# The products, copies and transfers of a batch laid out anew: first x turned by TensorE, q copied by ScalarE, three buffers of Q, K twice in the weight

## The reference, cut to what matters

```python
xn = layernorm(x)
q  = (xn @ Wq.T + bq) * 16 ** -0.5              # 16 x 512 x 256
k, v = split(xn @ Wkv.T + bkv)                  # 16 wide each
qr = q.reshape(16, 16 * 512, 16)                # 8192 rows of queries a batch
attn = softmax(qr @ k.T) @ v                    # the bulk: 8192 x 512 a batch
out_a = attn.(heads back) @ Wo.T + bo
tokens = einsum('elr,erc->elc', A, B)           # 6 experts x 100 tokens
a = softmax(xn @ tokens.T / 16)                 # kept for the chosen expert only
delta = (a[..., 1:] @ val[1:] + xn) @ wd.T + wd_b
out_f = xn + log(exp(delta * scale))            # of the chosen expert
result = x + out_a + out_f
```

## Time and profile before

| | |
|---|---|
| median of 3 timed runs | 1049.19 us (1047.77 to 1050.99) |
| profiled execution, its own time | 1037.82 us |
| its span, first to last instruction | 1036.0 us |
| TensorE busy | 892.1 us, 86% |
| VectorE busy | 812.0 us, 78% |
| ScalarE busy | 661.6 us, 64% |
| GpSimd busy | 515.6 us, 50% |
| mean granted clock of TensorE | 0.937 |

### The profile page before, as it was taken

How to read it: one execution, slowest core, us unless ns; L and a number is a source line. 1 busy time by engine, 2 the same in 40 slices (tenths; PEclk the granted TensorE clock), 3 DMA queues, 4 the chain that set the end, 5 groups by cost and what they waited for, 6 DMA issues and landing times.

```text
span 1036.0 us, 17715 instructions
## 1 busy us (share of the span) xinstructions
PE 892.1 (86%) x5837; PEld 287.0 (28%) x5837; DVE 812.0 (78%) x1523; ACT 661.6 (64%) x1334; POOL 515.6 (50%) x693
## 2 busy tenths in 40 slices
PE   1368988888999999898998898899899989989986
PEld 0223222322233232222223232223223223222222
DVE  5369898878889896888779787878878888877814
ACT  1003776766677685776667677667757767667882
POOL 1457375555557373555547455555636555532400
PEclk9766999989999998999899999989989999998988
DMA  4224144253524353253525326262533625241121
GB/s 121 60 55 67 56 76 97 74 103 93 87 85 91 105 94 89 82 104 94 95 65 90 102 82 110 87 94 67 90 94 81 114 83 104 61 77 52 54 67 37
DMA packets 128209, 86.56 MB, mean 84 GB/s; under 512 B 60279, under 2 KB 112248, under 8 KB 128120
## 3 DMA queue, kind: packets, MB, share of 16 engines
q1 hardware_dynamic: 128120, 85.43, 36.8%
HBM read 39.28 MB, written 33.54 MB: 70 GB/s over the span
## 4 chain that ended last, share of the span: by engine, by line
PE 53%; DMA 15%; DVE 14%; SPq 6%; ACT 4%; issue 4%; POOL 4%; POOLq 0%
PE pO L358 17%; PE pA L340 12%; DMA o_parts<-OTr 7%; DVE M L768 7%; DMA Lc<-o_parts 6%; PE pB L345 5%; SPq L993 5%; PE pA L483 4%; PE pA L412 3%; PE pA L465 3%; ACT P L585 2%; PE pA L452 2%; PE pA L401 2%; ACT OTr L591 2%; POOL KS L870 2%
## 5 line engine op out<-in xcount | busy, mean ns | idle before, releaser
L768 DVE TENSOR_REDUCE M<-pA 128x1 f32<-128x512 f32 x1024 | 644.6, 678 | 85.0 <-PE pA L340 83.2
L585 ACT ACTIVATE P<-pB 128x512 f32<-128x512 f32 x1002 | 556.7, 600 | 236.4 <-PE pB L345 227.5
L340 PE MATMUL pA<-K,Q 48*128 48x512 f16 x1024 | 342.0, 400 | 78.6 <-DVE M L768 66.9
L345 PE MATMUL pB<-Q,K 50*128 50x512 f16 x1002 | 333.8, 397 | 0.3 <-DVE M L768 0.3
L358 PE MATMUL pO<-P,VK 128*32 128x512 f32 x2048 | 287.1, 634 | 10.1 <-ACT P L585 7.9
L340 PEld LDWEIGHTS pA<-K,Q 48*128 48x128 f16 x1024 | 70.3, 95 | 432.8 <-DVE M L768 374.4
L925 POOL TENSOR_TENSOR On<-Op,Rb 128x512 f32<-128x512 f32 x31 | 39.9, 1287 | 178.2 <-DMA Rb<-l_parts 131.9
L876 POOL CAST Qp<-qf 128x512 f16<-128x512 f32 x32 | 19.5, 609 | 131.4 <-DVE qf L724 131.4
L911 POOL TENSOR_SCALAR Cz<-Cx 128x512 f32<-128x512 f32 x32 | 62.1, 1940 | 30.6 <-ACT Cx L567 30.5
L483 PE MATMUL pA<-wo,On 128*128 128x256 f32 x248 | 71.5, 413 | 3.3 <-DVE RL L781 1.9
L774 DVE RECIPROCAL Rc<-Lc 128x32 f32<-128x32 f32 x31 | 10.9, 353 | 79.5 <-DMA Lc<-o_parts 79.5
(11 more groups left out here) (144 smaller groups left out, 810.3 us busy)
## 6 DMA issues: line engine op xcount, KB each, us to landing
o_parts<-OTr SPq DMA_DIRECT2D x62, 256.0 KB, 2.1
Q<-q_pieces SPq DMA_DIRECT2D x90, 128.0 KB, 5.1
X<-in_x SPq DMA_DIRECT2D x16, 512.0 KB, 3.9
q_pieces<-Qp SPq DMA_DIRECT2D x32, 256.0 KB, 2.3
out<-OUT SPq DMA_DIRECT2D x32, 256.0 KB, 3.2
Op<-o_parts SPq DMA_DIRECT2D x31, 256.0 KB
Rb<-l_parts SPq DMA_DIRECT2D x31, 256.0 KB
K<-KS SPq DMA_DIRECT2D x96, 16.0 KB, 1.8
```

The lines of the kernel that those rows point to most:

```text
L340: e.matmul(bank1("ab", t)[:, :], Q16[r:r + 48, b % 2, h, 128 * s:128 * s + 128], K16[r:r + 48, b % 3, :], start=True, stop=True).then_inc( ...
L345: e.matmul(bankB(t)[:, :], K16[r:r + 50, b % 3, 128 * i:128 * i + 128], Q16[r:r + 50, b % 2, :, 32 * hh:32 * hh + 32], start=True, stop=Tr ...
L585: e.activation(P[:, u % PR, :], bankB(u + LB)[:, :], ACT.Exp, scale=alpha).then_inc(S("e"))
L768: e.tensor_reduce(M[:, t // 32 % 2, t % 2, t % 32 // 2:t % 32 // 2 + 1], bank1("ab", t)[:, :], AX, ALU.max, negate=True).then_inc(S("mx"))
```

## The change

**Start.** The first batch's normalized x is turned by eight TensorE transposes (`xt0`, `xt1`) instead of a DMA; ScalarE and VectorE split it out of PSUM. The upper pieces of the weights are made by ScalarE (`wh`, `wdh`) instead of VectorE. The reduction over Wq is ahead of the others (`rngq`). For batch 0 the split of q's first half is on VectorE, K's DMAs are issued by ScalarE, Q is read in two halves of four DMAs (`qra`, `qrb`), and the expert steps `s`, `p`, `a` stand at ticks 5, 13 and 17 instead of -21, 1.2 and 5.2.

**K and Q.** K's columns stand twice in the weight, so that `uk` gives 128 rows, of which K's 16 twice, and four DMAs copy K instead of six. `q_pieces` has the pieces inside the head, so four DMAs read Q instead of six; each half of q is written by two DMAs instead of one. `Q16` has three buffers, and qread waits for the batch three before. q is scaled out of PSUM by ScalarE.

**Ticks.** The steps with a product stand one to a group of four ticks. Beside the batch's tick, some move: kd from -46.2 to -42.6, q0 -57 to -53, qread -18.2 to -25.8, xtd -74.2 to -66.2, residual 2.3 to 9.1, rec +4, lw +4.2, rb +4.2, on +3.9 or +4, d1 23 to 3. ow and lr stay.

```diff
-U0, K0, V0, WC = C, C + ER, C + ER + D, C + ER + D + 32
-UKW = ER + D
+U0, K0, V0, WC = C, C + ER, C + ER + 2 * D, C + ER + 2 * D + 32
+UKW = ER + 2 * D
...
-    "root": -91.4, "refine": -90.2, "norm": -87.2, "pieces": -84.2, "xtd": -74.2,
-    "residual": 2.3, "q0": -57, "qe0": -55.4, "qs0": -53.8, "qw0": -50.2, "uk": -53, "uke": -51.4, "ks": -50.2,
-    "kd": -46.2, "vg": -49, "vge": -48.3, "q1": -45, "qe1": -43.4, "qs1": -42.2, "qw1": -38.2,
-    "vt": -41.1, "vte": -40.4, "gate": -38.8, "mask": -36.6, "mkd": -34.2,
-    "qread": -18.2, "utm": -27.2, "s": -21,
-    "smax": -20.4, "sexp": -18.8, "ssum": -17.4, "snorm": -16.2, "p": -12.9, "pte": -12.3, "a": -5, "mm": -4.4,
-    "d0": -1, "dexp0": -0.4, "d1": 23, "dexp1": 23.6, "guard0": 24.8, "dlog0": 29.2, "radd0": 30.8,
-    "d2": 39, "dexp2": 39.6, "d3": 47, "dexp3": 47.6, "guard1": 48.8, "dlog1": 53.2, "radd1": 54.8,
-    "o0": 131, "fo0": 131.6, "o1": 155, "fo1": 155.6, "st0": 157.2, "o2": 163, "fo2": 163.6, "o3": 183,
-    "fo3": 183.6, "st1": 185.2,
+    "root": -91.4, "refine": -90.2, "norm": -87.2, "ph": -82.4, "pl": -79, "xtd": -66.2,
+    "residual": 9.1, "q0": -53, "qe0": -51.4, "qs0": -47.5, "qw0": -45, "uk": -49, "uke": -47.4, "ks": -45.2,
+    "kd": -42.6, "vg": -45, "vge": -44.3, "q1": -41, "qe1": -39.4, "qs1": -38.2, "qw1": -35.6,
+    "vt": -37, "vte": -36.4, "gate": -34.8, "mask": -32.6, "mkd": -31.4,
+    "qread": -25.8, "utm": -24.9, "s": -21,
+    "smax": -20.4, "sexp": -18.8, "ssum": -17.4, "snorm": -16.2, "p": -13, "pte": -12.4, "a": -5, "mm": -4.4,
+    "d0": -1, "dexp0": -0.4, "d1": 3, "dexp1": 3.6, "guard0": 4.8, "dlog0": 9.4, "radd0": 14.8,
+    "d2": 39, "dexp2": 39.6, "d3": 47, "dexp3": 47.6, "guard1": 51.7, "dlog1": 56.2, "radd1": 57.6,
+    "o0": 135, "fo0": 135.6, "o1": 159, "fo1": 159.6, "st0": 163.2, "o2": 163, "fo2": 163.6, "o3": 183,
+    "fo3": 183.6, "st1": 188.6,
...
-    "q1": -54, "qe1": -53.9, "qs1": -53.6, "qw1": -50.1, "qread": -38, "p": 1.2, "pte": 1.8, "a": 5.2, "mm": 5.8,
-    "d0": 9.2, "dexp0": 9.8,
+    "q0": -57, "qe0": -56, "qs0": -55, "qw0": -54, "uk": -53, "uke": -52, "ks": -51, "kd": -50, "q1": -52, "qe1": -51,
+    "qs1": -50, "vg": -50, "vge": -49, "vt": -48, "vte": -47, "gate": -46, "mask": -45, "qw1": -40, "mkd": -39,
+    "utm": -30, "s": 5, "smax": 5.6, "sexp": 6.2, "ssum": 6.8, "snorm": 7.4, "p": 13, "pte": 13.6, "a": 17, "mm": 17.6,
+    "d0": 21, "dexp0": 21.6, "d1": 25, "dexp1": 25.6, "guard0": 26.8, "dlog0": 30.2, "radd0": 31.6,
...
-PARTH = {"lr": 66.2, "or": 66.3, "rec": 68.8, "lw": 69.4, "rb": 72.2, "on": 78.3}
+PARTH = {"lr": (82.2, 114.2), "or": (82.3, 114.3), "rec": (88.8, 120.8), "lw": (89.6, 121.4), "rb": (92.4, 124.4),
+         "on": (98.2, 130.3)}
+PARTH_LAST = {"lr": 86.2, "or": 86.3, "rec": 88.8, "lw": 89.4, "rb": 92.2, "on": 98.3}
...
+                for c in range(2):
+                    if due(f"xt{c}", n) is not None:
+                        w.wait_ge(*before2(f"xt{c}", 0))
+                        w.wait_ge(S("id"), 4)
+                        for i in range(4):
+                            w.wait_ge(S("xn"), i + 1)
+                            mm = e.transpose(bank2(f"xt{c}", 0)[:, 128 * i:128 * i + 128], XN[:, i, 128 * c:128 * c + 128],
+                                             idf[:, :])
+                        mm.then_inc(S("xtp"))
...
+                if due("wh", n) is not None:
+                    w.wait_ge(S("scl"), 1)
+                    w.wait_ge(S("wq"), 16)
+                    e.activation(wqP[:, 0, :, :], wq[:, :, :], ACT.Identity, scale=scl[:, 3:4]).then_inc(S("wqp"))
+                    w.wait_ge(S("wc"), 16)
+                    e.activation(wcP[:, 0, :, U0:WC], wc[:, :, U0:WC], ACT.Identity, scale=scl[:, 3:4]).then_inc(S("wcp"))
...
+                        e.activation(qf[:, g, :], bank1(f"q{g}", b)[:, :], ACT.Identity, scale=scl[:, 5:6],
+                                     bias=bq_s[:, g:g + 1]).then_inc(S(f"qe{g}"))
...
-                        e.tensor_scalar(qf[:, g, :], bank1(f"q{g}", b)[:, :], scl[:, 5:6], bq_s[:, g:g + 1],
-                                        ALU.mult, ALU.add).then_inc(S(f"qe{g}"))
...
-                    w.wait_ge(S("kc"), 2)
-                    w.wait_ge(S("b"), 64 * (b - 2))
-                    for k, piece in enumerate((0, 0, 1)):
-                        for a in range(2):
-                            p = 64 * a + 16 * k
-                            e.dma_start(K16[p:p + 16, b % 3, :], KS[96:112, piece, :]).then_inc(S("kd"), 16)
+                    if b > 2:
+                        w.wait_ge(S("b"), 64 * (b - 2))
+                    for a in range(2):
+                        e.dma_start(K16[64 * a:64 * a + 32, b % 3, :], KS[96:128, 0, :]).then_inc(S("kd"), 16)
+                        e.dma_start(K16[64 * a + 32:64 * a + 48, b % 3, :], KS[96:112, 1, :]).then_inc(S("kd"), 16)
...
-                        e.dma_start(qd[b % 2, :, 8 * g:8 * g + 8].rearrange("p h d t -> (h d) p t"),
-                                    Qp[:, g, :, :]).then_inc(S(f"qw_{g}"), 16)
+                        for k in range(2):
+                            e.dma_start(qd[b % 2, 8 * g:8 * g + 8, k], Qp[:, g, k, :]).then_inc(S(f"qw_{g}"), 16)
...
+                if (b := due("qread", n)):
+                    w.wait_ge(S("qw_0"), 32 * (b + 1))
+                    w.wait_ge(S("qw_1"), 32 * (b + 1))
+                    if b > 2:
+                        w.wait_ge(S("b"), 64 * (b - 2))
+                    for a in range(2):
+                        for p, pieces in ((0, 2), (32, 1)):
+                            e.dma_start(Q16[64 * a + p:64 * a + p + 16 * pieces, b % 3, :, :],
+                                        qd[b % 2, :, 0:pieces, :, 256 * a:256 * a + 256]
+                                        .rearrange("h k d t -> (k d) h t")).then_inc(S(f"qr_{b % 2}"), 16)
```

More of the change, by code:

```diff
@@ L119, in slots @@
                 put(name, 16 * g + slot + 4 * (g >= 4 * NB - 4), g)
-        if g % 2 and g < 4 * NB - 2:
-            for name, slot in PARTH.items():
-                put(name, 16 * g + slot + 4 * (g >= 4 * NB - 4), g // 2)
+    for nh in range(2 * NB - 1):
+        for name in PARTH:
+            put(name, 64 * (nh // 2) + (PARTH_LAST[name] if nh == 2 * NB - 2 else PARTH[name][nh % 2]), nh)
     return at
@@ L609, in _ @@
             for n in ticks(*DVE_NAMES):
-                if due("rng", n) is not None:
+                if due("rngq", n) is not None:
+                    e.memset(bmx[:, 2:3], 0.0).then_inc(S("wm"))
                     w.wait_ge(S("wq"), 16)
-                    w.wait_ge(S("ones"), 4)
-                    e.memset(bmx[:, 2:3], 0.0).then_inc(S("wm"))
                     e.tensor_reduce(wmx[:, 0:1], wq[:, :, :], XY, ALU.max,
                                     apply_absolute_value=True).then_inc(S("wm"))
+                if due("rng", n) is not None:
                     w.wait_ge(S("bq"), 16)
@@ L658, in _ @@
                     w.wait_ge(S("scl"), 1)
-                    e.tensor_scalar(wqP[:, 0, :, :], wq[:, :, :], scl[:, 3:4], None, ALU.mult).then_inc(S("wqp"))
+                    e.tensor_scalar(bq_s[:, :], bq_s[:, :], scl[:, 0:1], None, ALU.mult).then_inc(S("bqs"))
+                if due("wl", n) is not None:
                     w.wait_ge(S("wqp"), 1)
@@ L703, in _ @@
                     e.tensor_tensor(rstd[:, :], y4[:, :], y0[:, :], ALU.mult).then_inc(S("ry"))
-                if due("pieces", n) == 0:
-                    for k in range(2):
-                        w.wait_ge(S("xh0"), k + 1)
-                        e.tensor_tensor(XP[:, 2 * k:2 * k + 2, 1, :], XN[:, 2 * k:2 * k + 2, :],
-                                        XP[:, 2 * k:2 * k + 2, 0, :], ALU.subtract).then_inc(S("xl0"))
+                for c in range(2):
+                    if due(f"xl{c}", n) is not None:
+                        w.wait_ge(S("xh0"), c + 1)
+                        e.tensor_tensor(xT[:, 0, :, 1, c, :], bank2(f"xt{c}", 0)[:, :].rearrange("p (i t) -> p i t", t=128),
+                                        xT[:, 0, :, 0, c, :], ALU.subtract).then_inc(S("xl"))
                 if (b := due("uke", n)) is not None:
@@ L872, in _ @@
                 for g in range(2):
-                    if (b := due(f"qs{g}", n)) is not None:
+                    if (b := due(f"qs{g}", n)) is not None and b + g:
                         w.wait_ge(S(f"qe{g}"), b + 1)
-                        w.wait_ge(S(f"qw_{g}"), 16 * b)
+                        w.wait_ge(S(f"qw_{g}"), 32 * b)
                         e.tensor_copy(Qp[:, g, 0, :], qf[:, g, :]).then_inc(S(f"qh{g}"))
@@ L997, in _ @@
                         w.wait_ge(S(f"ql{g}"), b + 1)
[L998 to L1014 removed]
+                        w.wait_ge(S(f"qr_{b % 2}"), 64 * (b // 2))
@@ new lines, in _ @@
+                        for k in range(2):
+                            e.dma_start(qd[b % 2, 8 * g:8 * g + 8, k], Qp[:, g, k, :]).then_inc(S(f"qw_{g}"), 16)
```

(8 more changed lines are left out.)

136 lines of the change are left out of this document (68 added, 68 removed).

## The result

The changed kernel takes 922.09 us in the median (920.66 to 922.81), beside 1048.48 (1039.02 to 1050.99) of the kernel before: a ratio of 0.8807, interval 0.8751 to 0.8863. The prediction was 962 us, range 933 to 998: the sign was right, and the waits of the reciprocal and the half clock behind them went as it said, but the time was 40 us shorter than the forecast, 11 us outside its range. The span is 921.0 us.

What follows compares the result with a forecast made beforehand. TensorE was taken as near its bound, losing time to stops behind VectorE's reciprocal wait and the half clock; 102.5 + 13 x 54.2 = 807.1, plus 141.9 gave span 949.0, plus 13.2 gave 962 us, range 933 to 998.

Steps and rivals of the forecast that it cites:

- Batch 2's q product: Its first q product, at the end of the start, predicted at 102.5 instead of 116.4 us, bounds 98 and 109.
- Thirteen batches: First q product of batch 2 to batch 15's: 54.2 us a batch instead of 59.0, saving 62.7 us.
- From batch 15's q product to the end: The last stretch: 152.3 us before, less 7.1 and less 3.3, giving 141.9.
- From span to median: Old kernel's distance, median 1049.19 being 13.2 us above its span, added to the predicted span of 949.0.
- The idle time left in a batch: TensorE's idle time in a full batch, predicted to fall from 4.0 to 2.3 us, beside 51.9 busy.
- the two stops of the quickest batch: TensorE stops of 0.59 us behind the K scaling and 0.83 behind the gate's small steps, expected to remain.
- Rival 1: TensorE fills up, with hardly any idle time: 52.4 us a batch, 937 us in all; chance 0.17.
- The reciprocal's waits and the half clock: VectorE's waits for the sums, 1.07 and 3.28 us a batch, vanish, and half-clock stretches go if they follow the stops.
- The start: First q product at 16.4 us, first score tile 28, `utm` 32, batch 1's q product 45, batch 2's 57.5 later.
- The new wait that I named: SyncE at `load` waiting for GpSimd's residual of the batch ahead; taken at nothing, its appearance listed as a sign of error.
- rival 4: Slower: SyncE stands at `load` for the residual, delaying `ow` and the sums beyond 4 to 5 us slack; 1060 us; chance 0.03.
- The 1.7 us that the row of Rb would have added: Delay of the first score tile if the new q write took 4.05 us like Rb's read; kept inside the bounds.

Runs made afterwards that it cites:

- The kernel with the two main parts alone: Kernel before plus later reciprocal and three Q buffers with earlier read; start, product ticks and q's scaling as before: 968.15 us, ratio 0.9319.
- experiment 6: Changed kernel with the second batch prepared earlier (new ticks for batch 1): 917.00 us, then 916.01 beside 921.71 for the changed kernel.
- the kernel with one in every batch: Changed kernel with the second reciprocal of a batch due at tick 110.5 instead of 120.8: 1010.29 us, ratio 0.9732.
- Experiments 1 and 5: Kernel before plus later reciprocal: 972.45 us; plus three buffers, earlier read: 977.81; both: 968.15. Changed kernel, second reciprocal at tick 113.5: 945.87; at 110.5: 1010.29.

## Why the prediction was right or wrong

**The miss of 40 us in its terms.** Batch 2's q product: 102.5 predicted, 102.48 measured. Thirteen batches: 704.6 against 680.5, 24 us. From batch 15's q product to the end: 141.9 against 138.1, 4 us, half of it in the one batch that is left there. From span to median: 13.2 added, 1.1 measured, 12 us.

**The idle time left in a batch** is the step that failed: 51.9 busy, right (51.5), plus 2.3 of idle, of which 0.9 was there. I took the two stops of the quickest batch for a fixed cost, because their causes, the K scaling and the gate, are not removed. The row of the gate's last step in that very batch, 1.26 us for what takes 0.18, would have shown that a part of the second cause was GpSimd's pass beside it, and the change moves that pass (guard0 from 24.8 to 4.8). The kernel with the two main parts alone keeps both stops and takes 54.3, where I had 54.2; the ticks, which I priced at nothing ("the sum of TensorE's work is the same"), took 1.4 of it away, and q's scaling, priced at 0.2, took 0.6 once the ticks were there. Rival 1 named this and gave 52.4 us a batch, which is the number; it had 0.17.

**From span to median.** I carried 13.2 us over. The kernel before always took 1.8 us more than its span; the rest was that its runs differ. In its runs the time goes with the mean granted clock: 1023.02 us at 0.947, 1037.17 at 0.937, 1043.87 at 0.931. The profiled one, 1037.82, was quicker than the three timed beside it (1047.77 to 1050.99). The changed kernel has no stretches at the half clock in its batches, and its runs agree to 0.3%. By my own reason for the gain most of this distance should have gone too. The stretches in the batches are not all of it, though: the version of experiment 6 has none in its profile and ran from 913.5 to 919.55, and the kernel with one in every batch had runs within 4 us. With 1.8 the forecast would have been 951, rival 1 926.

**The reciprocal's waits and the half clock.** Right as mechanism: waits gone in both halves, `ow` to sums' read 2.1 us, no stretch at 0.5 from batch 2 to the last full one. Experiments 1 and 5 show both directions. The two parts are 4.7 of the 6.6 us a batch. The larger share is the stops themselves and not the clock: over the thirteen batches of the whole change TensorE's idle time fell from 71.3 to 13.5 us, 4.4 a batch, and its busy time from 696.0 to 667.0, 2.2 a batch.

**The start.** The sum was right by two misses that cancel. q at 16.06 (16.4 predicted). The first score tile at 30.85 instead of 28: K's four issues on ScalarE (to 26.7) hold up the V scaling behind them, and TensorE the `vt` transpose, 4.01 us, with the W2 products, at the half clock, behind that. I hadn't named what is queued behind those issues. The gate and the mask stand behind the V scaling too, so `utm` ended at 34.5 instead of 32, and batch 1's q product came 3 us late, at 47.95. From there to batch 2's it took 54.5 instead of 57.5; no run says why, so that the sum came out is luck.

**The queues.** The new wait that I named is there, SyncE for the residual, and it is free:

```profile
SPq L140 <- POOL Rs L901: 52.6, 14, 4.1
```

3.8 us in each of 14 batches. I had taken it at nothing and called it a sign of being wrong; it came and did no harm, since `ow`, due 4 ticks behind, then still has to wait for ScalarE's copy. It is within the 4 to 5 us of slack that rival 4 gave. The new q write can be seen at the start, where SyncE waits for its landing before it reads Q:

```profile
20.80 1.35 SPq L1039 DMA_DIRECT2D q_pieces<-Qp  x2
...
24.34 1.82 SPq L1046 DMA_DIRECT2D Q<-q_pieces  x4
```

The read goes out 2.2 us behind the second issue, 3.5 behind the first; I had 3.1 for both issues and the landing. The 1.7 us that the row of Rb would have added are not there. In the batches its 8 us of slack hide it.

**ScalarE.** An activation with scale and bias by partition out of PSUM took 773 ns where I took the 600 of the exponential; VectorE's took 802. ScalarE is busy 41.7 us of the 52.4, so it had room for it. The Trainium skill (ScalarE: Activation LUTs, What ACT_TABLE_LOAD costs) gives 186 ns + 0.833 ns a column with immediate scale and bias, and 93 more for each operand by partition; for 512 columns and two such operands that is an estimate of 799. The measured 773 lies 26 below it, and it would have been the better price.

## What to carry to other kernels

Where one engine is near its bound and works in a fixed order, the first thing to find is a small step that waits for a transfer in the order of an engine that others need; a later tick or an earlier transfer is worth the wait and, where one follows, the half clock behind it. Once it is gone, where the remaining small steps stand decides more than what they cost: a step moved to another engine gave 0.07 us a batch in the old order and 0.6 in the new one. And if the gain lies in what makes the runs differ, the distance from the profiled span to the median can't be carried over.
